# An expert loop with VectorE's and GpSimd's steps in another order, and its row loads moved from ScalarE's queue to SyncE's

## The reference

```
x = x + attn(layernorm(x))     # a long convolution along the 4096 positions, per channel
x = x + ffn(layernorm(x))      # two of 8 low-rank experts for each of 4096 tokens
# ffn, for expert e and the tokens routed to it:
h  = gelu(xr @ w1A[e].T @ w1B[e])         # 512 -> 64 -> 2048
ye = h @ w2A[e].T @ w2B[e]                # 2048 -> 64 -> 512
y[tok] += weight * ye
```

## Time and profile before

| | |
|---|---|
| median of 3 executions | 1114.91 us (1108.42 to 1119.63) |
| profiled execution, own time | 1123.56 us |
| its span, first to last instruction | 1121.8 us |
| mean granted TensorE clock | 0.933 |
| busy share of the span: PE, PEld, DVE, ACT, POOL | 81%, 68%, 73%, 70%, 53% |

### The profile page before, as it was taken

One profiled execution on the slowest core, in us unless ns is written; L12 is line 12 of the kernel. 1 busy time (PEld: TensorE's weight loads), 2 busy tenths in 40 slices (PEclk: granted clock), 3 DMA queues, 4 the chain that ended last, 5 costly groups with the idle time before them and its releaser, 6 DMA issues. The chain is left out here.

```text
span 1121.8 us, 32819 instructions
## 1 busy us (share of the span) xinstructions
PE 908.9 (81%) x11452; PEld 765.3 (68%) x11452; DVE 818.6 (73%) x1360; ACT 783.4 (70%) x1151; POOL 592.9 (53%) x642
## 2 busy tenths in 40 slices
PE   3760888888778788998989999899987888885881
PEld 2540676777667677787878788778876777774771
DVE  7878898979789333576756676776667989895891
ACT  3872898979779545655556566566677989896890
POOL 5625986868584133464656575657655323332330
PEclk9995899989989899999999999999998989998996
DMA  9998999999999896999999999899759989999976
GB/s 307 396 400 304 253 253 236 283 226 307 298 284 328 242 274 155 260 256 290 266 249 238 244 240 240 219 235 246 186 123 265 215 216 272 242 294 289 306 183 150
DMA packets 392136, 288.01 MB, mean 257 GB/s; under 512 B 125928, under 2 KB 339592, under 8 KB 391554
## 3 DMA queue, kind: packets, MB, share of 16 engines
q1 hardware_dynamic: 346018, 211.68, 69.1%
q0 software_dynamic: 19520, 36.26, 15.5%
q10 hardware_dynamic: 26528, 39.14, 9.9%
HBM read 197.41 MB, written 100.61 MB: 266 GB/s over the span
## 5 line engine op out<-in xcount | busy, mean ns | idle before, releaser
L1512 PE MATMUL ps<-xn,wb 128*128 128x128 f32 x2048 | 276.7, 291 | 0.0
L1512 PEld LDWEIGHTS ps<-xn,wb 128*128 128x128 f32 x2048 | 252.0, 201 | 17.5 <-issue 3.1
L598 POOL TENSOR_TENSOR cen<-xb,mean 128x512 f32<-128x512 f32 x128 | 143.1, 1119 | 219.2 <-DVE state L1316 142.5
L1114 ACT ACTIVATE cen<-ps 128x1024 f32<-128x1024 f32 x118 | 117.9, 1024 | 149.2 <-PE ps L1607 130.8
L1289 DVE TENSOR_TENSOR xn<-cen,rstd 128x1024 f32<-128x1024 f32 x128 | 174.6, 1364 | 49.7 <-POOL cen L598 37.0
L1607 PE MATMUL ps<-carry,wb 64*128 64x256 f32 x1248 | 163.5, 404 | 30.8 <-DVE carry L1362 25.5
L1499 PE MATMUL ps<-xn,near 128*32 128x128 f32 x2048 | 86.8, 289 | 119.3 <-DVE xn L1289 72.6
L1607 PEld LDWEIGHTS ps<-carry,wb 64*128 64x128 f32 x1248 | 126.0, 198 | 69.8 <-issue 44.7
L1300 DVE TENSOR_TENSOR xb<-xb,ps 128x1024 f32 (+1 forms) x128 | 152.8, 1194 | 9.9 <-PE ps L1524 9.9
L1011 ACT ACTIVATE wb<-wide 32x1024 f32<-32x1024 f32 x126 | 144.6, 1147 | 15.2 <-DMA wide<-taps_d 12.7
L1499 PEld LDWEIGHTS ps<-xn,near 128*32 128x32 f32 x2048 | 52.2, 112 | 142.1 <-issue 65.8
(11 more groups left out here) (179 smaller groups left out, 1349.3 us busy)
## 6 DMA issues: line engine op xcount, KB each, us to landing
xb<-L_attn_x SPq DMA_DIRECT2D x160, 512.0 KB, 9.9
out<-xb SPq DMA_DIRECT2D x72, 512.0 KB, 6.5
xb<-L_attn_x ACTq DMA_DIRECT2D x128, 256.0 KB
out<-xb SPq DMA_DIRECT2D x88, 256.0 KB, 4.7
wb<-L_ffn_w_B SPq DMA_DIRECT2D x78, 256.0 KB
wide<-taps_d SPq DMA_DIRECT2D x63, 256.0 KB, 5.9
dk<-decay_d SPq DMA_DIRECT2D x63, 128.0 KB, 4.8
out<-y_d SPq DMA_DIRECT2D x4, 1536.0 KB, 12.6
```

The lines of the kernel that those rows point to most:

```text
L598: pool.tensor_tensor(cen[:, k, 0:QB // 2].rearrange("p b r d -> p r b d"), unit_view(pool, g, i, k)[:, :, 0:UC // 2] .rearrange("p r (b d) ...
L1114: act.activation(act_at(q, b).rearrange("p f t -> p (f t)"), ps[:, 2 * (b % 2):2 * (b % 2) + 2, :].rearrange("p a t -> p (a t)"), ACT.Gelu ...
L1512: ins = pe.matmul(ps[:, QB * k + b, d * P:(d + 1) * P], wb[:, h, k * QB + b, d, :], xn[:, k, 2 * b + d, :], start=(b > 0 and d == 0), stop ...
```

## The change

In the loop of the experts

- VectorE's order becomes `rank_out`, `stage_down`, `normal`, `stage_out`, `rows2(q, 0)`, `rows2(q, 2)`, `rank_in_half(q+1)`, `token_stats(q+2)`: the statistics of the gathered tokens go from the middle of the tile to its end, behind `rank_in_half`, and the row statistics go behind `stage_out`;
- GpSimd's order becomes `deviation(q+1)`, `scatter(q-3)`, `gather(q+3)`: each tile's `deviation` goes from the end of one tile to the head of the next, and so behind the `picked` of a round where one lies between;
- the four row loads of a tile are issued by SyncE, between the up weights of two tiles, and no longer by ScalarE. SyncE waits for a pair of `ring2` buffers to be free before it issues the pair.

```diff
 # GpSimd
             def tile(q, m, first, rows):
                 k = m % 2
+                if is_in(q, NQ - 1):
+                    deviation(q + 1, 1 - k)
...
                 if is_in(q, NQ - 3):
                     gather(q + 3, 1 - k, None if isinstance(q, int) else (m + 3) % 4)
-                if is_in(q, NQ - 2):
-                    deviation(q + 2, k)
...
             deviation(0, 0)
-            deviation(1, 1)
 # SyncE
+            def row_loads(q):
+                for i in range(LR2):
+                    at = P + (q - ROW0) * LR2 + i
+                    if not isinstance(q, int):
+                        at = sp.snap(at)
+                    if i % 2 == 0:
+                        pair = (q - ROW0) * 2 + i // 2
+                        now(sp, pair - 1)
+                        wait(sp, s_free2, pair - 1)
+                    sp.dma_start(ring2[:, i], x_rows[:, bass.ds(at, 1), :].rearrange("s r d -> s (r d)"))\
+                      .then_inc(s_load2[i], 16)
...
             for j in range(YP, PIECES):
                 up_load(5 + j - YP, (5 + j) % 2)
+                row_loads(4 + j - YP)
                 sp.wait_ge(s_outb, 16 * j)
                 store_last(j)
             up_load(5 + PIECES - YP, 1)
-            with sp.Fori((6 + PIECES - YP) // 2, (NQ - 1) // 2) as p:
+            row_loads(4 + PIECES - YP)
+            with sp.Fori((6 + PIECES - YP) // 2, (ROW0 + TT) // 2) as p:
                 for k in range(2):
                     up_load(p * 2 + k, k)
-            up_load(NQ - 1, 0)
+                    row_loads(p * 2 + k - 1)
+            up_load(ROW0 + TT, 0)
+            row_loads(ROW0 + TT - 1)
+            for q in range(ROW0 + TT + 1, NQ):
+                up_load(q, q % 2)
 # ScalarE
-                if rows:
-                    rows2(0)
-                    rows2(2)
 # VectorE
-                if rows:
-                    rows2(q, 0)
-                if is_in(q, NQ - 2):
-                    token_stats(q + 2, k)
...
                 stage_out(q, e)
                 if rows:
+                    rows2(q, 0)
                     rows2(q, LR2 // 2)
                 if is_in(q, NQ - 1):
                     rank_in_half(q + 1)
+                if is_in(q, NQ - 2):
+                    token_stats(q + 2, k)
```

More of the change, by code:

```diff
@@ L1074, in gelu_table @@
                 act.activation(spare[:, 0:1], eps[:], ACT.Gelu)
[L1076 to L1084, removed]
             def stage_up(q):
@@ L1092, in tile @@
             def tile(q, m, first, rows):
-                def rows2(i0):
-                    for i in range(i0, i0 + 2):
-                        load2((q - ROW0) * LR2 + i, i, (q - ROW0) * 2 + i // 2)
                 if is_in(q, NQ - 1):
                     stage_up(q + 1)
-                if rows:
-                    rows2(0)
-                    rows2(2)
                 for b in range(4):
```

## The result

The changed kernel is slower: 1137.41 us median (1134.48 to 1139.79, 4 runs) against 1117.27 for the kernel before (1108.42 to 1123.22, 4 runs). The ratio is 1.0186, 95% interval 1.0109 to 1.0262, so about 20 us. The forecast was 1117 us with a range of 1099 to 1132. The profiled execution took 1136.16 us against 1123.56, 12.6 us more.

A forecast was written before the change was run, and what follows sets the result against it. TensorE was taken to set the expert loop's pace. Terms -33.3 + 32 + 3 = +2 us gave 1125.6 us against the profiled 1123.6, and 1117 us as median; range 1099 to 1132.

The forecast's parts named there:

- the first term: TensorE's first `up` in the expert loop: all 12 stalls behind `rank_in_half` taken as removed, -33.3 us.
- step (2): First tile of each round: `deviation` behind the pick makes a 12.9 us chain between turns; +32 us over seven rounds.
- Step (1): VectorE between `rank_in_half` and `turn`: the moved statistics fit with about half a microsecond to spare; nothing added.
- the slower rival: Gather before a pick lands later, behind SyncE's weights and rows: chain 14.9 us, 1131 us in all; chance 0.25.
- (4): GpSimd's scatters, 10.24 us apart, put the next gather back by about half a microsecond: +3 us, between 0 and 8.
- The clock: TensorE behind stalls of 2 us or more: matmuls at the lower clock level, 1.75 us lost a stall.
- The faster rival: Gather before a pick lands as in the quickest round: stall 1.6 us, no clock loss, 1096 us; chance 0.19.
- step (3): New waits of SyncE for `ring2` and GpSimd for `token_stats`: nothing, or 1.2 us a tile at most for GpSimd.
- The base of the sum: Profiled execution's 1123.6 us plus 2 us; its difference to the median of 1114.9 carried over, giving 1117 us.
- Rows that are late on SyncE's queue: Rows queued behind up weights land late for VectorE, half the old `rank_in_half` loss kept: 1134 us; chance 0.06.

The follow-up runs named there:

- e1: The changed kernel with `deviation` ahead of the pick again, as in the kernel before: 1119.21 us, ratio 1.0019 to the kernel before.
- e2: The changed kernel with slot numbers copied in each tile instead of at the head of a round: 1105.52 us, ratio 0.9901 to the kernel before.
- e10: The changed kernel with the rows on SyncE's queue but issued later, at ScalarE's time of before: 1117.74 us, ratio 1.0016 to the kernel before.
- e4: The kernel before with only the row loads moved to SyncE's queue, both orders as before: 1116.74 us, ratio 1.0004.
- e3: The changed kernel with the row loads back on ScalarE's queue, both orders new: 1123.07 us, ratio 1.0040 to the kernel before.
- e8: The kernel before with VectorE's new order alone: 1117.59 us, ratio 1.0003.
- e5: The kernel before with GpSimd's new order alone: 1122.42 us, ratio 1.0066.
- e12: The changed kernel with row loads of half the columns, issued at the same places: 1126.12 us, ratio 1.0093 to the kernel before.

## Why the prediction was wrong

**Where the loss goes.** Right: the first term removed all 12 stalls behind `rank_in_half`, and the stall went where step (2) put it, ahead of `turn` in the first tile of each of the seven rounds, behind `deviation`, behind the pick. e1 shows that `deviation`'s place is needed for it, e2 that the pick is. Step (1) held too: no other tile of the rounds waited for `normal`.

**The price of step (2).** Wrong in size. The chain from turn to turn was to be 12.9 us and took 14.1. The step from the copy to `deviation` is 0.32 us, not the 0.7 that I took, which is 0.4 in the change's favour. But the copy follows its `turn` by 11.34 us and not by 9.67: the gather is issued 0.6 us later (2.57 us behind its `turn` in the mean, 1.97 before), and from there to the copy it takes 8.77 us instead of 7.70. The prediction took that landing from the kernel before although the change moves the rows, and left their effect to the slower rival, at a quarter. That rival was the case: in e10, where the rows leave at their old time, the two are back at 2.06 and 7.74 us. It put the chain too high, 14.9 us against 14.1, since it had the landing at 7.2 us behind the issue where 6.35 came of it, just short of the 6.5 from which it was to decide; and it still came out lower in time, 1131 us, by the points below. The seven tiles with a stall cost 28.5 us where steps (2) and (4) had 23 without the clock; in the stall shown above the gather followed its scatter at once, 2.50 us behind its `turn`, where it was 1.97 in the quickest round before: half a microsecond, as (4) said.

**The clock.** 1.75 us a stall was nearly right here: 13.6 us for seven, 1.9 each. The threshold of about 2 us idle was wrong. In e10 an idle time of 1.89 us was followed by the loss and one of 2.52 was not, and in e4 a stall of 3.25 us was followed by none, so the length of the idle time alone doesn't decide it. TensorE's timeline of e4, in which that tile takes 489.92 - 476.54 = 13.38 us, no more than an undisturbed one and the stall:

```profile
476.54 1.09 PE L1581 MATMUL ps<-ident,wide 128*128 128x128 f32 x8 [0.82 <-DVE wide L1356]
...
485.40 2.00 PE L1608 MATMUL ps<-carry,wb 64*128 64x256 f32 x16 [3.25 <-DVE carry L1363]
...
489.92 1.09 PE L1581 MATMUL ps<-ident,wide 128*128 128x128 f32 x8
```

The faster rival's case, a stall that is short enough to leave the clock alone, does occur: in e3 and e10 the stalls, shorter than in the changed kernel, cost nothing beyond themselves in four of seven rounds.

**New waits, step (3).** Half right. SyncE's waits cost nothing (5.6 us of waits for rows). GpSimd's wait of `deviation` for the statistics cost nothing inside the rounds. At the loop's end it did, and I had not looked there: a second scatter is issued at the end of tile 36, and `deviation` queues behind it. GpSimd's timeline of the changed kernel:

```profile
822.90 1.53 POOL L560 DMA_INDIRECT out<-lag,slot_s  x1 [3.82 <-issue]
824.74 1.62 POOL L560 DMA_INDIRECT out<-lag,slot_s  x1 [0.30 <-issue]
825.82 0.82 POOL L648 TENSOR_SCALAR tstd<-tmean 128x2 f32<-128x2 f32 x1
```

The statistics for it were ready at 822.41 us. The last two tiles took 3.4 us more than 20.1, a cost that the sum didn't have. Not all of it is GpSimd's: 0.9 and 1.35 us are idle time ahead of the two `turn`, and the last tile took 11.1 us in e1 and e8 as well, which have VectorE's new order and GpSimd's old one.

**The base of the sum.** Wrong. The term removed, 33.3 us, is that of one execution, 1123.56 us, near the top of what the kernel before takes: its medians in the later comparisons were 1116 to 1119, its executions began at 1107.5. The kernel before varies by some 16 us from execution to execution, so the one that is profiled has its own loss, and I carried the difference over as if it had not. Profile against profile the change costs 12.6 us, median against median 20. The other kernels' traces point to the size. In e1, e4, e8 and e10, whose ratios are 1.0003 to 1.0019, the 33 tiles took 355.5 to 358.8 us, 24 to 27 us over 331.7, where the profiled execution before lost 33.6. If some 25 us is what the kernel before usually loses there, the changed kernel's 45.8 make about the 20 us that were measured. It isn't shown directly: one execution of the kernel before was traced, and the time outside these tiles differs between the traced executions too, from 752.8 to 763.5 us.

e3, with both new orders and the rows at their old time, is close to the kernel that the sum priced, and at 1.0040, 4.5 us, it came near the forecast's +2 us. That is partly luck: its 33 tiles lost 30.3 us where the sum had 35, and the kernel before some 25 where it had 33.3.

**The rest of the rivals.** The faster one, by GpSimd's larger share with one busy queue fewer, didn't happen: gathers landed later, and e10, with the same single queue, shows a landing of 5.33 us behind the issue, the same as before. The Trainium skill, DMA: Bandwidth & Descriptors, section "Issuing engines are not separate DMA queues", says that DMAs run on the same 16 engines whichever engine started them, and that starting them from several engines saves issue time only. The runs agree: e3 and e10, with the rows at the same time on ScalarE's and on SyncE's queue, gave 1.0040 and 1.0016, with intervals that overlap. Rows that are late on SyncE's queue weren't seen.

So the loss takes two parts of the change together: `deviation` behind the pick puts that gather's landing on TensorE's path, and rows that leave with the gather make it land later. Either undone gives 1.002 to 1.004 (e1, e10, e3), and neither by itself reaches 1.01 (e4 1.0004, e5 1.0066). The forecast failed by the size of two terms: the landing in step (2), and the 33.3 us to be removed. What stays open is what decides, from 1.9 to 3.3 us of idle time, whether the clock falls.

## What to carry to other kernels

Where a step is moved across a loop's boundary, look at what else stands on that boundary: a wait that happens once in four tiles and had room in the old order can become the chain that sets the pace. Rows that were issued earlier made the gather beside them land later here; ask which of the transfers that an earlier one will fly with has no slack before calling the earlier issue free. And when reordering only moves a stall, look for the wait that all orders share: copying the slot numbers in each tile instead of at the head of a round brought every version here to about 1% below the kernel before, while no order of the steps by itself came below it.

## What the runs showed of the hardware

- A gather that left together with 1 MB of row loads landed 6.35 us behind the end of its issue in the mean of seven; where they left behind it (e10), 5.33; with half of the bytes beside it (e12), 5.8. Each is from one execution. Which queue the rows were on made no difference that was measured (e3 1.0040, e10 1.0016).
- The clock's fall behind idle time cost 1.35 to 2.99 us in each of the changed kernel's seven stalls of 3.3 to 4.25 us, and about 1.7 us in three of seven stalls of 1.8 to 2.9 us in e10, the first three. In e4 nothing was lost behind 3.25 us.
